# Layer-1 output projection of a fused attention and expert kernel as three products of high and low parts

## What is computed

```python
def time_mix_layer(x, ln_w, ln_b, Wk, Wv, Wr, Wo):
    normed = layer_norm(x, ln_w, ln_b)
    k, v = normed @ Wk.T, normed @ Wv.T
    r = sigmoid(normed @ Wr.T)
    state[t] = 0.95 * state[t - 1] + 0.05 * k[t] * v[t]
    return x + (r * state) @ Wo.T          # Wo: the output projection
out = time_mix_layer(time_mix_layer(x, ...0), ...1)
x = layernorm(x + out)
x = layernorm(x + experts(x))              # top 2 of 8, each silu(x W1) * (x W2), then W3
```

## Time and profile before

| | us |
|---|---|
| median of 3 runs | 1155.1 |
| lowest and highest of them | 1153.98, 1155.54 |
| profiled execution, its own time | 1154.48 |
| span of its instructions in the profile | 1152.6 |
| TensorE busy | 1057.1 |
| VectorE busy | 902.6 |
| ScalarE busy | 633.2 |
| GpSimd busy | 656.2 |
| mean granted TensorE clock | 0.969 of full speed |

### The profile page before, as it was taken

The page is one execution under the profiler, slowest core; times in us unless marked ns, Lnnn a source line. Parts: engine busy times, 40 slices in busy tenths (PEclk is TensorE's granted clock), DMA queues, the critical chain, the costliest instruction groups (busy, mean ns, idle before and its releaser), DMA issues. The chain is left out here.

```text
span 1152.6 us, 22276 instructions
## 1 busy us (share of the span) xinstructions
PE 1057.1 (92%) x6690; PEld 929.6 (81%) x6690; DVE 902.6 (78%) x1990; ACT 633.2 (55%) x1101; POOL 656.2 (57%) x558
## 2 busy tenths in 40 slices
PE   6899999999999998789999999999999999999900
PEld 6688888787878786568889888988899999999900
DVE  5689998888888898676876677777778788888746
ACT  3355555555555554455454555565656666666528
POOL 2111545454555554566877676677647777777434
PEclk9899999999999999999999999999999999999955
DMA  4011222111121121656658678777877899999469
GB/s 184 18 43 69 56 56 56 56 55 55 55 55 55 55 56 38 184 155 160 136 102 216 166 194 207 180 222 177 222 191 192 248 260 235 241 243 237 90 213 388
DMA packets 81634, 167.76 MB, mean 146 GB/s; under 512 B 28224, under 2 KB 45504, under 8 KB 81312
## 3 DMA queue, kind: packets, MB, share of 16 engines
q1 hardware_dynamic: 51552, 131.41, 36.3%
q0 software_dynamic: 30016, 35.55, 16.7%
HBM read 121.82 MB, written 45.09 MB: 145 GB/s over the span
## 5 line engine op out<-in xcount | busy, mean ns | idle before, releaser
L883 POOL DMA_INDIRECT x_acc<-fy_sb,pair_out x135 | 253.3, 1876 | 118.8 <-DVE fy_sb L1149 41.6
L1430 PE MATMUL ring<-fxh,fw_hi 128*128 128x256 f32 (+1 forms) x720 | 235.0, 326 | 3.5 <-ACT fxh L742 2.2
L1432 PE MATMUL ring<-fxh,fw_lo 128*128 128x256 f32 (+1 forms) x720 | 232.9, 324 | 0.0
L1431 PE MATMUL ring<-fxl,fw_hi 128*128 128x256 f32 (+1 forms) x720 | 232.9, 323 | 0.0
L637 ACT ACTIVATE fw_hi<-w_raw 128x1024 fp32r<-128x1024 f32 x162 | 169.8, 1054 | 80.8 <-PE out L1501 80.0
L969 DVE TENSOR_TENSOR fw_lo<-w_raw,fw_hi 128x1024 fp32r<-128x1024 f32 x162 | 196.6, 1219 | 15.1 <-ACT fw_hi L637 14.9
L103 POOL DMA_INDIRECT xg<-x_src,pair_in x135 | 154.3, 1143 | 69.6 <-issue 49.0
L811 POOL TENSOR_TENSOR rs<-ve,neg_half 128x4 f32<-128x4 f32 x48 | 55.7, 1160 | 226.1 <-DVE nm L920 226.1
L1251 PE MATMUL ring<-xh,w_hi 128*128 128x512 f32 x384 | 161.5, 421 | 5.0 <-issue 3.3
L93 POOL DMA_INDIRECT slot_list<-pairs,slot_u x128 | 133.6, 1044 | 46.7 <-issue 32.4
L1499 PE MATMUL out<-fw_hi,gh 128*128 128x256 f32 x540 | 155.7, 288 | 1.1 <-DVE slot_u L1028 1.1
(11 more groups left out here) (154 smaller groups left out, 1990.3 us busy)
## 6 DMA issues: line engine op xcount, KB each, us to landing
w_raw<-w_ffn SPq DMA_DIRECT2D x162, 512.0 KB, 4.8
x_in<-h SPq DMA_DIRECT2D x16, 512.0 KB, 3.2
x_src<-x SPq DMA_DIRECT2D x16, 512.0 KB, 4.1
x_acc<-x SPq DMA_DIRECT2D x16, 512.0 KB, 5.1
acc<-x_acc SPq DMA_DIRECT2D x16, 512.0 KB, 7.4
out<-o SPq DMA_DIRECT2D x16, 512.0 KB, 6.2
xg<-x_src,pair_in POOLq DMA_INDIRECT x135
x_acc<-fy_sb,pair_out POOLq DMA_INDIRECT x135
```

Source lines behind the costliest of these rows:

```text
L883: nc.gpsimd.indirect_dma_start(x_acc, bass.IndirectOffsetOnAxis(pair_out[j][:, q, 0:1].bitcast(U32), 0), fy[j][:, q, :], None, compute_op= ...
L1430: nc.tensor.matmul(out, hi, rows_hi, start=dc == 0, stop=False)
L1431: nc.tensor.matmul(out, hi, rows_lo, start=False, stop=False)
L1432: last = nc.tensor.matmul(out, lo, rows_hi, start=False, stop=dc == DC - 1)
```

## The change

Layer 1's output projection, until now one f32 product per tile, becomes three fp32r products as in the other matrix products of this kernel: y_hi with the high part of the weights, y_hi with their low part, and y_lo with their high part. For this

- w_out keeps layer 2's weights only; layer 1's lie in w_out_parts as w_out_hi (ScalarE's copy, to fp32r) and w_out_lo (a new subtraction on VectorE, low_out, after keep_bias(0));
- in every step from 0 to 15 ScalarE makes y_hi, a copy of y[0] to fp32r, before keep_gates, and GpSimd makes y_lo = y[0] - y_hi between rstd(2, ...) and the sixth scatter;
- TensorE waits for y_lo (s_y_lo) in place of y (s_y[0]); gated waits for s_y_lo of the chunk before in place of its output product;
- y_hi and y_lo lie in the third part of the experts' first weight buffers; to make room, pad moves into u (so add_input of step 1 waits for the four stores) and the experts' second result buffer fy[1] moves onto x1T.

```diff
@@ -69,6 +69,7 @@
 PART = ((0, DC * H), (DC * H, 2 * DC * H), (2 * DC * H, WCOLS))
 SCAT = 16 * 2 * Q
 RANK_AT = 64
+OUT_AT = 61
...
@@ -234,7 +235,10 @@
         expert_no = sb("expert_no", [P, 2, Q, E])
 
         w_raw = w_raw_all[:, 0:LAYERS * DC * 4 * D].rearrange("p (l c m) -> p l c m", l=LAYERS, c=DC)
-        w_out = sb("w_out", [P, LAYERS, DC, D])
+        w_out = sb("w_out", [P, DC, D])
+        w_out_parts = sb("w_out_parts", [P, 2 * DC * D + 64], F32R)
+        w_out_hi = w_out_parts[:, OUT_AT:OUT_AT + DC * D].rearrange("p (c d) -> p c d", c=DC)
+        w_out_lo = w_out_parts[:, OUT_AT + DC * D:OUT_AT + 2 * DC * D].rearrange("p (c d) -> p c d", c=DC)
...
@@ -276,6 +280,8 @@
         sb("gap_w0", [P, 96])
         fw_hi, fw_lo, fy = [sb("fw_hi0", [P, WCOLS], F32R)], [sb("fw_lo0", [P, WCOLS], F32R)], [sb("fy_sb0", [P, Q, D])]
 
+        y_hi, y_lo = (part[0][:, PART[2][0]:PART[2][1]].rearrange("p (c t) -> p c t", c=DC) for part in (fw_hi, fw_lo))
...
             def early(name, shape, dt=F32):
@@ -288,7 +294,8 @@
             xh = [early(f"xh{l}", [P, DC, CH], F32R) for l in range(2)]
             xl = [early(f"xl{l}", [P, DC, CH], F32R) for l in range(2)]
             xr = early("xr", [P, Q, D])
-            pad = early("pad", [P, SLOTS // P, 2], I32)
+            pad = (u[:, :, :, :].rearrange("p a q d -> p (a q d)")[:, 0:2 * SLOTS // P].bitcast(I32)
+                   .rearrange("p (n c) -> p n c", c=2))
...
@@ -298,7 +305,7 @@
         gh, gl = [sb("gh0", [P, HC * CH], F32R)], [sb("gl0", [P, HC * CH], F32R)]
         gh.append(sb("gh1", [P, HC * CH], F32R))
         gl.append(sb("gl1", [P, HC * CH], F32R))
-        fy.append(sb("fy_sb1", [P, Q, D]))
+        fy.append(x1T[:, :, :].rearrange("p c t -> p (c t)").rearrange("p (q d) -> p q d", q=Q))
...
@@ -327,6 +334,7 @@
         s_sn = [sem("scanned0"), sem("scanned1")]
         s_cy = [sem("carried0"), sem("carried1")]
         s_y = [sem("y_ready0"), sem("y_ready1")]
+        s_y_hi, s_y_lo = sem("gated_hi"), sem("gated_lo")
...
@@ -431,7 +439,10 @@
             eng.wait_ge(s_sn[l], n * 2 + e + 1)
             eng.wait_ge(s_r[l], n * 2 + e + 1)
             if within(n, 1, CHUNKS):
-                eng.wait_ge(s_po[l], n * 2)
+                if l == 0:
+                    eng.wait_ge(s_y_lo, n)
+                else:
+                    eng.wait_ge(s_po[l], n * 2)
             eng.tensor_tensor(y[l][:, e, :], state[l][:, e, :], r_sb[l][:, e, :], ALU.mult).then_inc(s_y[l], 1)
...
@@ -463,7 +474,7 @@
                 for l in range(LAYERS):
                     sp.wait_ge(s_bias, l + 1)
                     sp.wait_ge(s_whi[l], DC + 1)
-                    sp.wait_ge(s_wlo[l], DC)
+                    sp.wait_ge(s_wlo[l], DC if l else DC + 1)
...
@@ -558,7 +569,8 @@
                 for dc in range(DC):
                     nc.scalar.activation(w_hi[:, l, dc, 0:3 * D], w_raw[:, l, dc, 0:3 * D], ACT.Copy,
                                          scale=lnp[:, 0, l, dc:dc + 1]).then_inc(s_whi[l], 1)
-                nc.scalar.activation(w_out[:, l, :, :], w_raw[:, l, :, 3 * D:4 * D], ACT.Copy).then_inc(s_whi[l], 1)
+                w_out_copy = w_out[:, :, :] if l else w_out_hi
+                nc.scalar.activation(w_out_copy, w_raw[:, l, :, 3 * D:4 * D], ACT.Copy).then_inc(s_whi[l], 1)
...
@@ -677,6 +689,11 @@
                     act.wait_ge(s_biassb[1], 2)
                 if within(s, 3, CHUNKS + 2) and not at(s, CHUNKS) and not at(s, CHUNKS + 1):
                     keep_x1T(s)
+                if layer1:
+                    act.wait_ge(s_y[0], s * 2 + 2)
+                    if within(s, 1, CHUNKS):
+                        act.wait_ge(s_po[0], s * 2)
+                    nc.scalar.activation(y_hi, y[0][:, :, :], ACT.Copy).then_inc(s_y_hi, 1)
...
@@ -856,6 +873,9 @@
                 scatter(s, j, 4, 1)
                 if within(s, 2, CHUNKS + 1):
                     rstd(2, s - 2)
+                if layer1:
+                    pool.wait_ge(s_y_hi, s + 1)
+                    nc.gpsimd.tensor_tensor(y_lo, y[0][:, :, :], y_hi.bitcast(F32), ALU.subtract).then_inc(s_y_lo, 1)
                 scatter(s, j, 5, 1)
                 scatter(s, j, 6, 1)
                 scatter(s, j, 7, 1)
@@ -935,6 +955,12 @@
                                                    lnp[:, 0, l, dc:dc + 1], w_hi[:, l, dc, 0:3 * D].bitcast(F32),
                                                    ALU.mult, ALU.subtract).then_inc(s_wlo[l], 1)
 
+            def low_out():
+
+                dve.wait_ge(s_whi[0], DC + 1)
+                nc.vector.tensor_tensor(w_out_lo, w_raw[:, 0, :, 3 * D:4 * D], w_out_hi.bitcast(F32),
+                                        ALU.subtract).then_inc(s_wlo[0], 1)
...
@@ -953,6 +979,7 @@
             low_weights(0)
             x_lo(0, 0)
             keep_bias(0)
+            low_out()
             dve.wait_ge(s_x[1], 16)
             norm_stats(0, x_in[:, 1, :, :], 1)
...
@@ -1039,6 +1066,8 @@
 
             def add_input(s, j):
 
+                if at(s, 1):
+                    dve.wait_ge(s_padst, 64)
                 if within(s, 3, CHUNKS):
                     dve.wait_ge(s_z, s * 2 - 4)
                 nc.vector.tensor_tensor(u[:, 1 - j, :, :], xr[:, :, :], x_in[:, 1 - j, :, :], ALU.add).then_inc(s_u, 1)
@@ -1256,9 +1285,16 @@
             def output(l, out, q0, columns=(0, 1)):
                 for i in columns:
                     q = q0 + i
+                    to = out[:, i * D:(i + 1) * D]
                     for dc in range(DC):
-                        last = nc.tensor.matmul(out[:, i * D:(i + 1) * D], y[l][:, dc, q * P:(q + 1) * P],
-                                                w_out[:, l, dc, :], start=dc == 0, stop=dc == DC - 1)
+                        if l == 0:
+                            hi, lo = (part[:, dc, q * P:(q + 1) * P] for part in (y_hi, y_lo))
+                            nc.tensor.matmul(to, hi, w_out_hi[:, dc, :], start=dc == 0, stop=False)
+                            nc.tensor.matmul(to, hi, w_out_lo[:, dc, :], start=False, stop=False)
+                            last = nc.tensor.matmul(to, lo, w_out_hi[:, dc, :], start=False, stop=dc == DC - 1)
+                        else:
+                            last = nc.tensor.matmul(to, y[1][:, dc, q * P:(q + 1) * P],
+                                                    w_out[:, dc, :], start=dc == 0, stop=dc == DC - 1)
                 if columns[-1] == 1:
                     last.then_inc(s_po[l], 1)
...
@@ -1380,7 +1416,9 @@
                 if layer2:
                     project(1, s, s - 1, 1, j, (2,))
                 if layer1:
-                    pe.wait_ge(s_y[0], s * 2 + 2)
+                    if at(s, 0):
+                        pe.wait_ge(s_wlo[0], DC + 1)
+                    pe.wait_ge(s_y_lo, s + 1)
                     if within(s, 1, CHUNKS):
                         pe.wait_ge(s_res, s * 2)
```

## The result

The changed kernel takes 1182.7 us (median of 4 runs, 1182.25 to 1185.71) against 1155.3 us for the kernel before (4 runs, 1153.98 to 1155.87). The ratio is 1.0245, with a 95% interval of 1.0229 to 1.026: slower by 27.4 us. The forecast was 1177.5 us, with a range of 1156 to 1188.

The account below looks back on a forecast made before the run. VectorE's queue, looped through GpSimd's rstd and ScalarE's k_sb, was taken to set the step, with TensorE nearly full. 1154.5 + 19.2 (y_lo holding VectorE in 12 steps) + 3.8 (start) = 1177.5 us, range 1156 to 1188.

Parts of the forecast that it names:

- The bound: Attention steps of 28 us: VectorE's program sets the step, looped through GpSimd's rstd and ScalarE's k_sb; TensorE nearly full.
- TensorE's part at 0: Layer 1's output in each step: new products save 0.45 us, worth 0 on the path (bounds 0 and 6.8 us).
- ScalarE's part at 0: y_hi before keep_gates: a 1.05 us copy fits into 2.65 us of ScalarE's idle time, so costs 0.
- y_lo and what it meets: GpSimd's y_lo in the steps: takes 1.92 us and blocks VectorE's gap, which wants two SBUF operands.
- the hold: Steps 3 to 14: gap waits 1.60 us for y_lo to end, 19.2 us in all (7.7 to 29.5).
- my sum from memsets: y_lo's price: 0.20 us plus two streams of 1024 columns at 0.84 ns, 1.92 us (0.96 to 2.78).
- steps 1 and 2: No router work behind rstd, so y_lo costs 0 there, with 1.6 us each as bound.
- Step 15: VectorE first waits 2.23 us for the turned gates and y_lo is through by then, so no hold.
- The start: Step 0: first output starts at 35.1 for 30.66 (+4.4), its group 0.6 shorter: 3.8 us (1.0 to 4.6).
- VectorE isn't held: Rival, chance 0.22: y_lo stretches instead of holding VectorE in the steps; only the start costs, 1157.7 us (1155 to 1159).
- only by turns: Rival, chance 0.08: VectorE held for part of y_lo; start's 3.2 us and up to half of 19.2, 1159 to 1167.
- TensorE sets the step: Rival, chance 0.10: each output's 0.45 us saving counts in the steps, giving 1150.9 us, faster.

Follow-up runs that it names:

- kv first: Kernel before, with layer 1's first kv of steps 2 to 15 moved ahead of layer 2's second y on VectorE: 1146.4 us, ratio 0.9928; repeated 1146.0 us.
- f32 products: Changed kernel with layer 1's output again one f32 product per tile, y_hi, y_lo and w_out_lo still made: 1182.2 us, ratio 1.0239.
- the first experiment: Changed kernel with y_lo moved up in GpSimd's order, from behind rstd(2) to behind rstd(0), ahead of the fifth scatter: 1166.2 us, ratio 1.0093.

## Why the prediction was right, and where its sizes were off

**The bound.** VectorE's program sets the step, with the loop through GpSimd's rstd and ScalarE's k_sb in it: confirmed by two edits that leave TensorE's work alone (kv first, and y_lo moved) and by one that changes TensorE's and leaves the time as it is (f32 products).

**TensorE's part at 0.** Confirmed. The output now goes from 327.81 to the next product at 330.70, 2.89 us against 3.27 in the earlier trace rows, so it saves 0.38 us rather than the 0.45 forecast:

```profile
327.81 0.28 PE L1292 MATMUL out<-w_out_parts,fw_hi 128*128 128x256 f32 x1
...
330.70 0.40 PE L1280 MATMUL ring<-xh,w_hi 128*128 128x512 f32 x1
```

TensorE's waits grew by (28.5 - 5.1)/11 = 2.1 us a step, as foreseen. Only with kv first, where TensorE is busy nearly all the time, did the new products go with shorter steps (by 0.25 and 0.33 us), and no measured time has shown that gain.

**ScalarE's part at 0.** Confirmed: without y_lo the steps are as long as before. The idle time ahead of gate_cols shrank from 2.65 to 1.69 us and stayed a reserve:

```profile
316.56 1.06 ACT L696 ACTIVATE fw_hi<-y 128x1024 fp32r<-128x1024 f32 x1
319.32 0.28 ACT L621 ACTIVATE gate_cols<-out 128x128 f32<-128x128 f32 x1 [1.69 <-PE out L1331]
```

**y_lo and what it meets.** The mechanism and the count of 12 steps were right; the mis-sized term is the hold: 2.07 us a step in place of 1.60, so 24.9 us in place of 19.2. In step 10 the cast's hold alone is 2.22 - 0.20 = 2.02, and it differs from 1.60 by three things. y_lo takes 2.39 us, not 1.92: +0.47. It starts 0.15 us after nb's start, not 0.36 as the scatter did: -0.21. And it meets the cast, not gap: gap's usual place, 0.32 us behind the cast's start, would be 322.87, and it would have been held for 324.74 - 322.87 = 1.87 us, so the cast adds 0.15; 0.01 remains as rounding. Most of the miss is thus the price of y_lo. The Trainium skill's "GPSIMD Engine Reference", section 3, from which the prediction had an estimate of 2.25 us for y_lo, was nearer than my sum from memsets; the trace's 2.39 decides.

I had looked for VectorE instructions with two SBUF operands only, and so passed over the cast and ve, which have one. The held instructions were the cast (2.22 us), ve (0.50, in the first experiment), w_lo (3.10), the scan of step 2 (3.21) and y (1.57); statistics, their aggregation and FIND_INDEX8 weren't. For steps 1 and 2 the prediction had 0, because no router work stands behind rstd there; 0 is what they cost, but for step 2 by luck, since a hold of 1.93 us fell on a wait of 1.72. Step 15 was close, too: y_lo wasn't through when the gates came at 471.40, as the prediction had it, but ran from 470.56 to 472.97, beside the search for the best experts (MAX8 and FIND_INDEX8, at their usual lengths), and ended just as the cast began (472.93, 0.17 us). The Trainium skill, "SBUF — State Buffer", section "Who interferes with whom", lists cast and tensor_scalar among the instructions that can enter a two-port mode and then contend with GpSimd, when their operands meet certain conditions; the cast and ve agree with that here.

**The start.** Forecast 3.8 us, measured 3.0 at the second residual addition (40.24 against 37.23). y_lo didn't wait for w_lo: y_hi ended at 31.96, y_lo started at 32.04, 1.1 us earlier than forecast, and w_lo's second instruction, 0.06 us behind it, was held instead. That y_lo took 2.34 us and not 1.92 made up for 0.4 of it, so two misses cancel in part: the first output started at 34.75 (35.1 forecast). From there to the next product, at 40.00, its group took 5.25 us (5.6 forecast) at a granted clock of 0.50, the level of 1.2 GHz. The row of 34.7 to 40.3 us:

```profile
34.70:40.30 5.60, 5.55 (x25) 5.58 (x26) 1.25 (x3) 0.00 (x0) 0.00 (x0) 0.50 0.00 0
```

**The sum.** Measured in the trace: 24.86 + 3.10 + 0.67 (step 15) = 28.6 us; forecast: 19.2 + 3.8 = 23.0. The 0.67 stood in no term of the sum.

**The rivals.** That VectorE isn't held, or only by turns, falls with the cast ending 0.03 us behind y_lo, which itself is no longer than where it runs beside statistics (2.39 and 2.40 us). TensorE sets the step: falls with the f32 products.

## What to carry to other kernels

Before work goes to GpSimd, lay its length over VectorE's timeline at the place where it will stand, and look at every VectorE instruction there that reads SBUF, small ones and those with one input too: an eight-column cast cost 2 us a step, while statistics beside the same subtraction kept their length. Ask also what stands behind the held instruction: where a wait follows, as in step 2, the hold is free. Splitting a long GpSimd instruction and moving the halves beside instructions that aren't held gave back some 23 of the 27 us. And find what sets the step before making another engine faster: one VectorE instruction put earlier in the step gave 8 to 10 us, where the new products by themselves gave none.

## What the runs showed of the hardware that was not expected

- A VectorE cast with one SBUF input of 128x8 stood for 1.97 to 2.34 us beside GpSimd's subtraction in place of 0.17 to 0.23, twelve times in twelve, and its hold is recorded as its own length, not as a wait.
- Which engine starts first decides, in both directions: GpSimd's y_lo held the cast that started 0.20 us behind it, and GpSimd's nb took 0.20 us when it started 0.02 us ahead of VectorE's scan, and 1.24 us when it started 0.03 us behind it.
- A one-input tensor_scalar of 128x4 was held (0.49 to 0.59 us in steps 2 to 14 in place of 0.17), while statistics (0.41 us each), their aggregation (0.38) and FIND_INDEX8 (0.15) ran at their usual lengths beside GpSimd's subtraction.
- GpSimd's two-input subtraction took 2.34 to 2.41 us for 1024 columns and 1.26 to 1.33 us for 512, thus some 2.1 ns a column and 0.2 us besides.
